# A four-layer graph network on one core: twenty summed rows a turn, GpSimd's signed blocks as maximum times sign, and layer norms scaled by VectorE

## The chip, the cores and the metric

The kernel runs on one core of one Trainium2 chip. The metric is the device time of one execution in microseconds (us). The kernel before takes 5407.69 us, the median of three runs (5406.17 to 5408.93).

## The reference, cut to what matters

64 graphs (batches) of 256 nodes with 128 features go through four layers, each `x = x + layer(relu(layernorm(x)))`. The first layer, a pairwise attention, is by far the largest piece of work:

```python
h = jnp.maximum(_layernorm(x, axis=-1), 0.0)
s1, s2 = einsum('bkf,ef->bke', h, W1), einsum('bkf,ef->bke', h, W2)   # e has 256 channels; W1 and W2 are halves of adj
pre = s1[:, :, None, :] + s2[:, None, :, :] + b_lin                    # 256 x 256 x 256 values a graph
e = einsum('bije,e->bij', where(pre >= 0, pre, 0.2 * pre), a) + adj
x = x + sigmoid(einsum('bij,bjf->bif', softmax(e, axis=2), h))
```

Layers 2 to 4 are a message-passing layer, an attention layer and a gated recurrent layer of five steps. They are small beside the first.

## The kernel before, in words

Two graphs (a pair) are worked through per *turn*; 32 turns carry the first layer, and layers 2 to 4 of earlier pairs run in their gaps. A turn has 128 *lots* (`LOTS`), 64 for each graph. In layer 1 the leaky slope is split off, so that what is left of each row i and channel half c is `max(W, U_i)`: W is a 128 x 256 tile (channels on partitions, all nodes j along the free axis) and U_i is one column. One such 128 x 256 maximum is a *block*. A lot is eight blocks, four groups of two halves (`BLOCKS`), which go into one of twelve places of `ring` (each four tiles of 128 x 512). TensorE then multiplies the place with `a_window` (L1163): four matmuls of 32 columns each, side by side, each of them two passes in the profile, so eight matmul rows for a lot.

The blocks of a lot are shared out by hand among three engines: VectorE (DVE; L746 for one block, L751 for two or four in one instruction), GpSimd (POOL; L620) and ScalarE (ACT; L956). `Plan.share_blocks` does it greedily with a price for each block and each stage (L89 and `stage_costs`, in tenths of a us), so that the three engines' running sums stay level. Each engine's program is in order: per lot its blocks, then the stages of the other layers that are booked at that lot (the tables `POST`, `PRE`, `LN1` to `LN3`, `L1` to `L3`). An engine that refills a place waits for `freed` of that place, which TensorE raises after the matmuls of the lot twelve before. TensorE waits for `by_dve`, `by_act` and `by_pool` of the place.

*Summed rows.* For some rows (`SUMMED_ROWS`, six of 32, 2 x 6 = 12 a turn over its two graphs) both channel halves are added ahead of the matmul, so that such a row needs one lot instead of two; from turn 2 on a turn has 116 lots instead of 128. The sign of the second half relative to the first is a column `sigma` of plus and minus ones. GpSimd makes the *signed* block, sigma times the maximum (L610), as a clamp of `W_signed` between `U_floor` and `U_ceiling`; these are made from `U_signed` in L599 and L600, and `U_signed` and `W_signed` by ScalarE in L976 and L979. VectorE then does maximum and addition in one instruction (L742), always by VectorE, four blocks a summed lot. `signed` has two buffers of four blocks.

*Layer norms.* For each graph (`pre`) and for LN1 to LN3 of a pair VectorE takes the statistics (L767, L772, L802, L808), minus the mean (L776, L812) and the variance plus epsilon (L777, L813). GpSimd makes the power -1/2 (L582) and the product of it and minus the mean (L584). ScalarE scales, shifts and clips each 128 x 128 block at zero in one activation (L964 for `pre`, two blocks; L1006 for the others, four blocks). TensorE transposes the result and ScalarE copies the transpose out of PSUM (L968, L1014, L1041, L1061).

## Time and profile before

| what | value |
|---|---|
| median of three runs | 5407.69 us (5406.17 to 5408.93) |
| the profiled execution | 5412.65 us, its span 5410.9 us |
| matmul, busy | 5288.8 us (98%), 37702 instructions |
| VectorE, busy | 5225.0 us (97%), 10763 |
| ScalarE, busy | 5143.4 us (95%), 13517 |
| GpSimd, busy | 5080.7 us (94%), 9752 |
| granted TensorE clock | 0.996 of full speed |

All four engines are busy over nine tenths of the span in nearly every slice. The profiled execution lies 5 us over the median of the runs. A busy time is the union of an engine's instructions; neighbours on one engine overlap a little, so the mean length of an instruction is more than what one more of it costs. The steady part of the execution repeats with every turn: L982, which runs once for each graph, starts at 1617.99 us and, 40 executions and so 20 turns later, at 4931.72 us, which is 165.69 us a turn.

### The profile page before, as it was taken

What the parts mean: (1) busy time and instruction counts of PE and PEld (TensorE: products, weight loads), DVE (VectorE), ACT (ScalarE), POOL (GpSimd) and SP (SyncE); (2) the same over time, 40 slices, a digit from 0 to 9 for tenths busy, and PEclk for the clock granted to TensorE, in tenths of its full rate; (3) what the DMA queues carried; (4) which work ended last, traced back from release to release, by engine and by line L of the source; (5) the groups of instructions that cost most, each with busy time, mean ns of one, the idle gap of its engine ahead of it and who ended that gap; (6) DMA issues with size and microseconds to landing.
All of it is one profiled execution on the core that took longest, in us unless ns stands there. A gap on an engine that the chain in (4) does not pass through costs nothing.

```text
span 5410.9 us, 115261 instructions
## 1 busy us (share of the span) xinstructions
PE 5288.8 (98%) x37702; PEld 2060.9 (38%) x37702; DVE 5225.0 (97%) x10763; ACT 5143.4 (95%) x13517; POOL 5080.7 (94%) x9752
## 2 busy tenths in 40 slices
PE   8999999999999999999999999999999999999997
PEld 2333333333333333333334333333333333333334
DVE  9999999999999999999999999999999999999993
ACT  8999999999999999999999999999999999999993
POOL 8899999999999999999999999999999999999990
PEclk9999999999999999999999999999999999999998
DMA  0000000000000000000000000000000000000000
GB/s 15 3 4 7 7 6 3 6 7 7 6 7 3 6 7 7 6 3 6 7 7 6 7 3 6 7 7 6 3 6 7 7 6 7 3 6 7 7 5 6
DMA packets 44381, 34.00 MB, mean 6 GB/s; under 512 B 4752, under 2 KB 39696, under 8 KB 43792
## 3 DMA queue, kind: packets, MB, share of 16 engines
q1 hardware_dynamic: 43792, 26.63, 1.6%
q8 instruction: 311, 5.10, 0.4%
q14 instruction: 278, 2.28, 0.1%
HBM read 9.84 MB, written 8.39 MB: 3 GB/s over the span
## 4 chain that ended last, share of the span: by engine, by line
PE 52%; ACT 26%; DVE 20%; issue 2%; DMA 0%; POOL 0%; SPq 0%; DVEq 0%; POOLq 0%
PE S L1163 29%; ACT ring L956 20%; PE R L1108 9%; DVE ring L751 8%; PE S L1108 5%; DVE ring L742 4%; PE W L1108 3%; DVE ring L746 2%; PE R L1301 2%; PE V L1108 1%; ACT h L1006 1%; DVE rh L890 1%; DVE gated L898 1%; DVE diff L894 1%; DVE h3T L902 1%
## 5 line engine op out<-in xcount | busy, mean ns | idle before, releaser
L956 ACT ACTIVATE ring<-V,U_minus 128x256 f32<-128x256 f32 x10681 | 4338.4, 850 | 1.6 <-issue 1.6
L1163 PE MATMUL S<-ring,a_window 128*32 128x512 f32 x29888 | 3401.9, 596 | 51.0 <-DVE ring L746 21.4
L620 POOL TENSOR_SCALAR ring<-W,U 128x256 f32<-128x256 f32 x6362 | 3175.7, 518 | 12.1 <-ACT V L982 11.8
L751 DVE TENSOR_TENSOR ring<-U,W 128x512 f32<-128x512 f32 (+1 forms) x2884 | 2536.1, 903 | 7.3 <-ACT V L982 7.3
L1163 PEld LDWEIGHTS S<-ring,a_window 128*32 128x32 f32 x29888 | 886.5, 109 | 2294.5 <-issue 2052.1
L610 POOL TENSOR_SCALAR signed<-W_signed,U_ceiling,U_floor 128x256 f32<-128x256 f32 x2880 | 1699.6, 594 | 6.3
L742 DVE SCALAR_TENSOR_TENSOR ring<-W,U,signed 128x256 f32<-128x256 f32 x2880 | 1193.8, 471 | 0.0
L746 DVE TENSOR_TENSOR ring<-U,W 128x256 f32<-128x256 f32 x1747 | 711.4, 409 | 0.0
L1108 PE MATMUL R<-mT,W 128*128 128x512 f32 (+1 forms) x640 | 334.9, 605 | 16.3 <-ACT mT L1068 16.3
L1108 PE MATMUL R<-AT,h 128*128 128x256 f32 x1264 | 311.9, 390 | 2.1 <-ACT h L1080 2.1
L582 POOL TENSOR_TENSOR rstd<-var,minus_half 128x4 f32<-128x4 f32 (+1 forms) x160 | 144.0, 900 | 141.2 <-DVE var L813 125.6
L1108 PEld LDWEIGHTS R<-AT,h 128*128 128x128 f32 x1264 | 230.6, 193 | 78.4 <-issue 50.3
L890 DVE SCALAR_TENSOR_TENSOR rh<-tr,h3T 128x512 f32<-128x512 f32 (+1 forms) x164 | 165.1, 1007 | 58.3 <-ACT tr L1071 58.3
L1074 ACT ACTIVATE tz<-R,bias 128x512 f32<-128x512 f32 (+1 forms) x160 | 161.1, 1007 | 52.4 <-PE R L1301 52.3
L1006 ACT ACTIVATE h<-X,shift,rstd 128x128 f32<-128x128 f32 x384 | 193.8, 870 | 6.8 <-POOL shift L584 6.8
L1080 ACT ACTIVATE h<-R 128x512 f32<-128x512 f32 (+1 forms) x128 | 131.8, 1029 | 69.5 <-PE R L1309 69.5
L1108 PEld LDWEIGHTS R<-mT,W 128*128 128x128 f32 x640 | 110.5, 192 | 172.0 <-ACT mT L1068 93.7
L1068 ACT ACTIVATE mT<-R 128x512 f32<-128x512 f32 (+1 forms) x160 | 165.0, 1031 | 11.0 <-PE R L1108 11.0
L1301 PE MATMUL R<-mT,W 128*128 128x512 f32 (+1 forms) x320 | 168.5, 608 | 0.0
L1071 ACT ACTIVATE tr<-R,bias 128x512 f32<-128x512 f32 (+1 forms) x160 | 157.6, 985 | 9.6 <-PE R L1108 9.6
L1077 ACT ACTIVATE cand<-R,bias 128x512 f32<-128x512 f32 (+1 forms) x160 | 164.7, 1029 | 0.7 <-PE R L1108 0.7
L1108 PE MATMUL R<-h3T,turned 128*128 128x512 f32 (+1 forms) x320 | 162.6, 590 | 0.0
(185 smaller groups left out, 4512.9 us busy)
## 6 DMA issues: line engine op xcount, KB each, us to landing
X<-in_x SPq DMA_DIRECT2D x64, 128.0 KB, 2.1
X_held<-X SPq DMA_DIRECT2D x32, 256.0 KB, 2.3
out<-OUT SPq DMA_DIRECT2D x64, 128.0 KB, 1.9
edge<-in_L_gnn_w_w SPq DMA_DIRECT2D x3, 128.0 KB, 2.2
A<-in_adj SPq DMA_DIRECT2D x1, 256.0 KB, 2.7
Wn<-in_L_gnn_Wn SPq DMA_DIRECT2D x1, 128.0 KB, 2.9
Wm<-in_L_gnn_Wm SPq DMA_DIRECT2D x1, 128.0 KB, 3.0
weight<-in_L_gnn_u_w SPq DMA_DIRECT2D x2, 64.0 KB, 2.2
```

What stands on the lines that cost most here:

```text
L610: made = gp.tensor_scalar(signed[:, number % 2, at], W_signed[:, y], U_ceiling[:, y, i:i + 1], U_floor[:, y, i:i + 1], ALU.min, ALU.max)
L620: last = gp.tensor_scalar(ring[:, place, g, half * N:(half + 1) * N], W[:, y, c], LARGEST, U[:, y, c, i:i + 1], ALU.min, ALU.max)
L742: piece = dve.scalar_tensor_tensor(ring[:, place, g, half * N:(half + 1) * N], w, U[:, y, c, i:i + 1], signed[:, number % 2, at], ALU.max, ...
L746: piece = dve.tensor_tensor(ring[:, place, g, half * N:(half + 1) * N], U[:, y, c, i:i + 1].to_broadcast([P, N]), w, ALU.max)
L751: piece = dve.tensor_tensor(ring[:, place, g:g + groups].rearrange("p g (h j) -> p g h j", h=NB), u.unsqueeze(3).to_broadcast([P, groups, ...
L890: dve.scalar_tensor_tensor(rh[:, cols_], tr[:, cols_], 1.0, h3T[:, cols_], ALU.add, ALU.mult).then_inc(rh_ready, 1)
L956: last = act.activation(ring[:, place, g, half * N:(half + 1) * N], W_scalar[y][:, c * N:(c + 1) * N], ACT.Relu, bias=U_minus[:, y, c, i:i ...
L1006: last = act.activation(dst[:, r], src[:, r], ACT.Relu, bias=shift[:, n, r:r + 1], scale=rstd[:, n, r:r + 1])
L1068: act.activation(mT[:, cols_], messages[:, cols_], ACT.Copy).then_inc(mT_ready, 1)
L1108: return pe.matmul(dst, lhsT, rhs, start=start, stop=stop)
L1163: last = pe.matmul(S[y][g * ROWS:(g + 1) * ROWS, :], a_window[:, c, ROWS - 1 - row:2 * ROWS - 1 - row], ring[:, place, g], start=False, st ...
L1301: pe.matmul(gates[:, cols_], W345[:, 0], mT[:, cols_], start=False, stop=True, skip_group_check=True).then_inc(z_psum, 1)
```

## The change

Three things change. First, ten rows of 32 are summed instead of six (`SUMMED_COUNT = 10`, twenty a turn): from turn 2 on a turn has 108 lots. The two sides of a lot begin at rows 22 and 21, so that their summed lots do not meet. Secondly, GpSimd makes a signed block from `W` and `U` directly, as maximum with `U_i`, then times `sigma`; the clamps, `U_signed`, `W_signed` and what they need go, and `signed` has three buffers. Thirdly, a layer norm's subtraction and scaling move from ScalarE to VectorE, one instruction per 128 x 128 block with two per-partition scalars. For LN1 and LN2 the clip at zero goes into ScalarE's copy out of PSUM; for `pre` and LN3 it is one more VectorE instruction over the whole tile. GpSimd makes the power only. The planner's stage prices follow, and its block prices stay.

```diff
-SUMMED_EVERY, SUMMED_AT = 5, 2
-SUMMED_ROWS = [row for row in range(ROWS) if row % SUMMED_EVERY == SUMMED_AT]
-FIRST_ROW = (0, 30)
+SIGNED = 3
+SUMMED_COUNT = 10
+SUMMED_ROWS = [(2 * n + 1) * ROWS // (2 * SUMMED_COUNT) for n in range(SUMMED_COUNT)]
+FIRST_ROW = (22, 21)
...
-            put(vector, PRE[h], half, stats=7.0)
-            put(scalar, PRE[h], half, norm=7.7, copy=2.7, evacuate=32)
-            put(pool, PRE[h], half, factors=12)
-            if self.has_sums:
-                book(pool, half, 11)
+            put(vector, PRE[h], half, stats=6.1, norm=6.6)
+            put(scalar, PRE[h], half, copy=2.7, evacuate=26)
+            put(pool, PRE[h], half, factors=8)
         if self.turn:
             for ln in (LN1, LN2, LN3):
-                put(vector, ln, 0, stats=12.5)
-                put(scalar, ln, 0, norm=15.4, copy=4.8)
-                put(pool, ln, 0, factors=12)
+                put(vector, ln, 0, stats=11.3, norm=11.8 if ln is LN3 else 7.9)
+                put(scalar, ln, 0, copy=4.8)
+                put(pool, ln, 0, factors=10)
...
                 gp.tensor_tensor(rstd_, var_, minus_half[:, 0:width], ALU.pow).then_inc(sem_rstd, 1)
-                gp.wait_ge(sem_rstd, value)
-                gp.tensor_tensor(shift_, minus_mean_, rstd_, ALU.mult).then_inc(sem_shift, 1)
...
-                    if turn.plan.has_sums:
-                        gp.tensor_scalar(U_floor[:, y], U_signed[:, y], sigma_limit[:], None, ALU.min)
-                        gp.tensor_scalar(U_ceiling[:, y], U_signed[:, y], sigma_limit[:], None, ALU.max).then_inc(clamps_ready, 1)
...
-                    if at == 0 and number >= 2:
-                        taken = divmod(number - 2, len(turn.plan.sum_lots))
+                    if at == 0 and number >= SIGNED:
+                        taken = divmod(number - SIGNED, len(turn.plan.sum_lots))
...
-                    made = gp.tensor_scalar(signed[:, number % 2, at], W_signed[:, y], U_ceiling[:, y, i:i + 1], U_floor[:, y, i:i + 1], ALU.min, ALU.max)
+                    made = gp.tensor_scalar(signed[:, number % SIGNED, at], W[:, y, 1], U[:, y, 1, i:i + 1], sigma[:], ALU.max, ALU.mult)
...
-                    dve.tensor_scalar(minus_mean0[:], mv0[:, :, 0], -1.0, None, ALU.mult)
                     dve.tensor_scalar(var0[:], mv0[:, :, 1], LN_EPS, None, ALU.add).then_inc(pre_eps, 1)
+                if p == PRE[1 - y]["norm"]:
+                    dve.wait_ge(pre_rstd, value)
+                    for r in range(NB):
+                        last = dve.tensor_scalar(H0[:, y, r], X0[:, y, r], mv0[:, r, 0:1], rstd0[:, r:r + 1], ALU.subtract, ALU.mult)
+                    last.then_inc(pre_scaled, 1)
+                    one_piece()
+                    dve.wait_ge(pre_scaled, value)
+                    dve.tensor_scalar(H0[:, y], H0[:, y], 0.0, None, ALU.max).then_inc(h0_ready, 1)
...
-                    dve.tensor_scalar(minus_mean[:, n], mv[:, n, :, 0], -1.0, None, ALU.mult)
+                if t == ln["norm"]:
+                    dve.wait_ge(ln_rstd[n], pair)
+                    for r in range(4):
+                        last = dve.tensor_scalar(dst[:, r], src[:, r], mv[:, n, r, 0:1], rstd[:, n, r:r + 1], ALU.subtract, ALU.mult)
+                    if n < 2:
+                        last.then_inc(h_ready[n], 1)
+                    else:
+                        last.then_inc(ln3_scaled, 1)
+                        one_piece()
+                        dve.wait_ge(ln3_scaled, pair)
+                        dve.tensor_scalar(dst[:], dst[:], 0.0, None, ALU.max).then_inc(h_ready[n], 1)
...
-                        last = act.activation(H0[:, y, r], X0[:, y, r], ACT.Relu, bias=shift0[:, r:r + 1], scale=rstd0[:, r:r + 1])
...
-                    act.activation(U_signed[:, y].rearrange("p (b k) -> p b k", k=len(SUMMED_ROWS)),
...
-                    act.activation(W_signed[:, y], W_bank[y][:, N:2 * N], ACT.Identity, scale=sigma[:])
...
-                        last = act.activation(dst[:, r], src[:, r], ACT.Relu, bias=shift[:, n, r:r + 1], scale=rstd[:, n, r:r + 1])
...
-                    act.activation(h1T[:], S[1][:], ACT.Copy).then_inc(hT_ready[0], 1)
+                    act.activation(h1T[:], S[1][:], ACT.Relu).then_inc(hT_ready[0], 1)
...
-                    act.activation(h2T[:], W_bank[0][:], ACT.Copy).then_inc(hT_ready[1], 1)
+                    act.activation(h2T[:], W_bank[0][:], ACT.Relu).then_inc(hT_ready[1], 1)
```

## Rows read from the trace of the kernel before

**Rows 1.** The page's busy times by engine, and its chain that ended last.
```profile
PE 5288.8 (98%) x37702; PEld 2060.9 (38%) x37702; DVE 5225.0 (97%) x10763; ACT 5143.4 (95%) x13517; POOL 5080.7 (94%) x9752
PE 52%; ACT 26%; DVE 20%; issue 2%; DMA 0%; POOL 0%; SPq 0%; DVEq 0%; POOLq 0%
```
**Rows 2.** Busy us per engine in a stretch of ten turns: PE, PEld, DVE, ACT, POOL.
```profile
1644.00:3301.00 1657.00, 1635.40 (x11701) 635.68 (x11700) 1630.99 (x3361) 1604.82 (x4223) 1605.19 (x3062) 1.00 0.02 6
```
**Rows 3.** Groups of the whole span: busy us, mean ns | idle before, releaser.
```profile
L956 ACT ACTIVATE ring<-V,U_minus 128x256 f32<-128x256 f32 x10681 | 4338.4, 850 | 1.6 <-issue 1.6
L1163 PE MATMUL S<-ring,a_window 128*32 128x512 f32 x29888 | 3401.9, 596 | 51.0 <-DVE ring L746 21.4 <-issue 21.2 <-ACT ring L956 3.1
L620 POOL TENSOR_SCALAR ring<-W,U 128x256 f32<-128x256 f32 x6362 | 3175.7, 518 | 12.1 <-ACT V L982 11.8 <-issue 0.3
L610 POOL TENSOR_SCALAR signed<-W_signed,U_ceiling,U_floor 128x256 f32<-128x256 f32 x2880 | 1699.6, 594 | 6.3
L751 DVE TENSOR_TENSOR ring<-U,W 128x1024 f32<-128x1024 f32 x1225 | 1455.0, 1211 | 0.0
L742 DVE SCALAR_TENSOR_TENSOR ring<-W,U,signed 128x256 f32<-128x256 f32 x2880 | 1193.8, 471 | 0.0
L751 DVE TENSOR_TENSOR ring<-U,W 128x512 f32<-128x512 f32 x1659 | 1110.3, 675 | 7.3 <-ACT V L982 7.3
L746 DVE TENSOR_TENSOR ring<-U,W 128x256 f32<-128x256 f32 x1747 | 711.4, 409 | 0.0
```
**Rows 4.** Some of the waits of the same ten turns: us in total, times, longest.
```profile
PEld S L1163 <- DVE ring L746: 40.8, 41, 1.4
POOL edge_sum L635 <- DVE edge L840: 23.6, 10, 2.5
POOL rstd L582 <- DVE var L813: 21.4, 30, 1.7
ACT h L1080 <- PE R L1309: 16.7, 20, 1.4
DVE X L850 <- PE S L1108: 13.0, 10, 1.3
```
**Rows 5.** Timeline, from the start, of back-to-back runs on three engines (start us, us).
```profile
2399.94 7.08 PE L1163 MATMUL S<-ring,a_window 128*32 128x512 f32 x64
...
2400.23 1.65 DVE L742 SCALAR_TENSOR_TENSOR ring<-W,U,signed 128x256 f32<-128x256 f32 x4
...
2410.20 2.78 PE L1163 MATMUL S<-ring,a_window 128*32 128x512 f32 x24
```
**Rows 6.** From the longest pieces of the critical chain: start us, us.
```profile
1630.34 6.93 ACT ring L956 x19
```
**Rows 7.** Two groups of the ten turns that the change removes.
```profile
L599 POOL TENSOR_SCALAR U_floor<-U_signed,sigma_limit 128x48 f32<-128x48 f32 x20 | 8.4, 419 | 0.0
...
L584 POOL TENSOR_TENSOR shift<-minus_mean,rstd 128x4 f32<-128x4 f32 x30 | 6.0, 199 | 2.3
```
**Rows 8.** Timeline: ScalarE's evacuation at the start, and one layer norm at the end.
```profile
15.04 0.41 ACT L976 ACTIVATE U_signed<-V,sigma_b,sigma 128x48 f32<-128x48 f32 x1
...
15.67 0.63 ACT L980 ACTIVATE W<-W 128x512 f32<-128x512 f32 x1
...
5318.31 1.65 ACT L1006 ACTIVATE h<-X,shift,rstd 128x128 f32<-128x128 f32 x4 [2.44 <-POOL shift L584]
```
**Rows 9.** VectorE's instructions with one SBUF input, whole span, by form.
```profile
L813 DVE TENSOR_SCALAR var<-mv 128x4 f32<-128x4 f32 x96 | 16.3, 170 | 0.0
...
L670 DVE TENSOR_SCALAR neg_score<-A,a_abs 128x256 f32<-128x256 f32 x2 | 0.6, 350 | 0.0
```
**Rows 10.** Timeline of VectorE and GpSimd side by side: L610 under L818.
```profile
2503.58 0.43 DVE L818 TENSOR_SCALAR exp<-exp 128x512 f32<-128x512 f32 x1
2503.66 0.77 POOL L610 TENSOR_SCALAR signed<-W_signed,U_ceiling,U_floor 128x256 f32<-128x256 f32 x1
```
**Rows 11.** L610 by itself: duration ns min/median/max.
```profile
L610 POOL TENSOR_SCALAR signed<-W_signed,U_ceiling,U_floor x2880: 539/553/1602, 301.8 to 5264.1; 128x256 f32<-128x256 f32 x192
```

More of the change, by code:

```diff
@@ L219, in spare_blocks @@
         for h in range(2):
-            for at in (POST[h]["transpose"], PRE[h]["stats"], PRE[h]["stats"]):
+            for at in (POST[h]["transpose"], PRE[h]["stats"], PRE[h]["stats"], PRE[h]["norm"]):
                 spare[h * LOTS_B + at] += 1
@@ L223, in spare_blocks @@
             spare[ln["stats"]] += 2
+        spare[LN3["norm"]] += 1
         for at in (L1["elu"], L1["recv_elu"], L2["residual"]):
@@ L258, in node @@
         return half * P + g * ROWS + self.entry(t, n)[0]
-    def signed_node(self, t, n):
-        g, half = group_half(n)
-        return (half * GROUPS + g) * len(SUMMED_ROWS) + SUMMED_ROWS.index(self.entry(t, n)[0])
 PLANS = [Plan(turn) for turn in range(3)]
@@ L369, in gnn_stack @@
         U_minus = sb("U_minus", [P, 2, EC, N])
[L370 to L374 removed]
+        signed = sb("signed", [P, SIGNED, SIDE_BLOCKS, N])
         W = sb("W", [P, 2, EC, N])
@@ L449, in gnn_stack @@
         freed = [sem(f"freed{n}") for n in range(RING)]
-        x_loaded, pre_stats, pre_mv, pre_eps, pre_rstd = (sem(n) for n in "x_loaded pre_stats pre_mv pre_eps pre_rstd".split())
-        pre_shift, h0_ready, h0T_psum, h0T_ready = (sem(n) for n in "pre_shift h0_ready h0T_psum h0T_ready".split())
-        clamps_ready, signed_ready = sem("clamps_ready"), sem("signed_ready")
+        x_loaded, pre_stats, pre_mv, pre_eps, pre_rstd, pre_scaled = (sem(n) for n in "x_loaded pre_stats pre_mv pre_eps pre_rstd pre_scaled".split())
+        h0_ready, h0T_psum, h0T_ready = (sem(n) for n in "h0_ready h0T_psum h0T_ready".split())
+        signed_ready = sem("signed_ready")
         uw_psum, u_ready, w_ready, u_evacuated = (sem(n) for n in "uw_psum u_ready w_ready u_evacuated".split())
@@ L463, in gnn_stack @@
         ln_rstd = [sem(f"ln{n}_rstd") for n in (1, 2, 3)]
-        ln_shift = [sem(f"ln{n}_shift") for n in (1, 2, 3)]
+        ln3_scaled = sem("ln3_scaled")
         h_ready = [sem(f"h{n}_ready") for n in (1, 2, 3)]
@@ L742, in one_piece @@
                     piece = dve.scalar_tensor_tensor(ring[:, place, g, half * N:(half + 1) * N], w, U[:, y, c, i:i + 1],
-                                                     signed[:, number % 2, at], ALU.max, ALU.add)
+                                                     signed[:, number % SIGNED, at], ALU.max, ALU.add)
                 elif end - first == 1:
@@ L826, in layer1 @@
                     dve.wait_ge(x1_ready, turn.at(2, 0))
-                stats(t, LN1, 0, X1, pair)
+                layer_norm(t, LN1, 0, X1, h1, pair)
                 if t == L1["elu"]:
@@ L881, in layer3 @@
                         dve.wait_ge(x3_ready, turn.at(1, 0))
-                    stats(t, LN3, 2, X3, turn.at(1, 0))
+                    layer_norm(t, LN3, 2, X3, h3, turn.at(1, 0))
                 pair, s, p = layer3_at(turn, t)
@@ L913, in _ @@
             pre(PRE[1]["stats"], 0, 1)
+            pre(PRE[1]["norm"], 0, 1)
             setup_layer0()
@@ L960, in pre @@
             def pre(p, y, value):
-                if p == PRE[1 - y]["norm"]:
-                    act.wait_ge(pre_shift, value)
-                    for r in range(NB):
-                        last = act.activation(H0[:, y, r], X0[:, y, r], ACT.Relu, bias=shift0[:, r:r + 1], scale=rstd0[:, r:r + 1])
-                    last.then_inc(h0_ready, 1)
                 if p == PRE[1 - y]["copy"]:
@@ L999, in post @@
                     last.then_inc(tanh0_ready, 1)
-            def norm(t, ln, n, src, dst, pair):
-                if t == ln["norm"]:
-                    act.wait_ge(ln_shift[n], pair)
-                    for r in range(4):
-                        last = act.activation(dst[:, r], src[:, r], ACT.Relu, bias=shift[:, n, r:r + 1], scale=rstd[:, n, r:r + 1])
-                    last.then_inc(h_ready[n], 1)
             def layer1(t, turn):
                 pair = turn.at(1, 0)
-                norm(t, LN1, 0, X1, h1, pair)
                 if t == LN1["copy"]:
                     act.wait_ge(hT_psum[0], pair)
-                    act.activation(h1T[:], S[1][:], ACT.Copy).then_inc(hT_ready[0], 1)
+                    act.activation(h1T[:], S[1][:], ACT.Relu).then_inc(hT_ready[0], 1)
                 if t == L1["exp"]:
@@ L1057, in layer3 @@
                 if turn.has_l12:
-                    norm(t, LN3, 2, X3, h3, turn.at(1, 0))
                     if t == LN3["copy"]:
```

37 lines of the change are left out of this document (9 added, 28 removed).

## The prediction

> **What bounds the kernel now.** I read the page first, then a stretch of whole turns, then who waited for whom. The page shows four engines busy for 94 to 98% of the span, and a chain that runs half over the matmuls [rows 1]. That alone would name TensorE as the bound, and the change would then be a gain, since it takes matmuls away. The rows on the ring say otherwise. If TensorE set the pace, the three engines that fill the ring would stand before a place that isn't free yet. In the whole span the five forms of ring instruction have idle time before them of 1.6 (ScalarE), 12.1 (GpSimd), 7.3, 0 and 0 us (VectorE), and the two large ones of these are one wait each for L982, at the very start [rows 3]. No fill ever waits for `freed`. The other way round there are waits: in ten turns TensorE's weight loads of the ring wait 41 times, 40.8 us in all, for VectorE's block [rows 4]. So the three filling engines set the pace and TensorE follows. Its own work shows it too: 64 ring matmuls back to back take 7.08 us and 24 take 2.78 [rows 5], so one costs 4.30 / 40 = 0.1075 us and a lot of eight 0.86 us; a turn of 116 lots is 99.8 us of ring matmul, where the busy time of L1163 is 3401.9 us over some 32 turns, 106 us each [rows 3]. About 6 us a turn of what looks busy is waiting under latency.
>
> How full are the three? In ten turns, 1657 us, VectorE is busy 1631.0, ScalarE 1604.8 and GpSimd 1605.2 us [rows 2]: per turn of 165.7 us that leaves 2.6, 5.2 and 5.2 us idle (rounded). Of GpSimd's 5.2 us, 2.4 + 2.1 are waits for VectorE (L840, L813) [rows 4]. VectorE is the fullest; 1.3 of its 2.6 us are a wait for a matmul of layer 2 (L850) [rows 4]. ScalarE waits for matmuls too, the largest 1.7 us a turn (L1080) [rows 4]. These waits are all that a lighter TensorE can give back.
>
> **The counts.** Followed through with the new constants, `share_blocks` gives for a turn from turn 2 on: summed blocks on VectorE 96 to 160, plain VectorE blocks in instructions of four 38 to 25, of two 50 to 34, of one 52 to 46; GpSimd's plain blocks 194 to 131, its signed blocks 96 to 160; ScalarE's blocks 334 to 359. The old counts agree with the trace: 30 x 96 = 2880 L742 and 2880 L610 [rows 3]. Turns 0 and 1 have no sums and change by under 2 us together.
>
> **TensorE.** Eight lots fewer: 8 x 0.86 = 6.9 us a turn less, 206 us over 30 turns. I put this at nothing, because it is work beside the filling engines; it only moves TensorE's slack from some 6 to some 13 us a turn.
>
> **VectorE, blocks.** Four L742 take 1.65 us together and one 0.471 [rows 3, 5], so the next one starts after 0.393 us: neighbours overlap by 0.08 us. With the same overlap off the means of [rows 3], an instruction of four blocks costs 1.13, of two 0.60, of one 0.33 us. The change: -13 x 1.13 - 16 x 0.60 - 6 x 0.33 + 64 x 0.393 = -14.7 - 9.6 - 2.0 + 25.2 = -1.1 us a turn.
>
> **VectorE, layer norms.** Sixteen instructions of 128 x 128 with two column scalars (four in `pre`, twelve in LN1 to LN3), two clips of 128 x 256 and one of 128 x 512. None of that form is in the trace. One of 4 elements takes 0.170 us, one of 256 with one column scalar 0.350 [rows 9], and one of 512 without 0.43 [rows 10]. Halfway between the first two is 0.26 for 128 elements; a second column scalar may add something; less the overlap that is 0.18 to 0.27, and I take 0.22, near the middle. The clips: 0.23 and 0.36. Sum 16 x 0.22 + 2 x 0.23 + 0.36 = 4.3 us. Five small instructions for minus the mean go, at 0.09 each (0.170 less the overlap) [rows 9], 0.5 us. Net +3.8 us, bounds +3.1 and +4.6. The new waits for `rstd` I price at nothing: in 30 cases GpSimd waited for VectorE's variance [rows 4], so it arrives two lots ahead and makes its power (mean about 1 us) before VectorE has done the next lot or two; if that lead is lost, each costs up to 1 us with all of VectorE's later pieces behind it, and L1's projection too.
>
> VectorE in all: +2.7 us a turn, 163.1 to 165.8.
>
> **ScalarE.** 19 blocks of L956 take 6.93 us [rows 6], 0.365 each: +25 x 0.365 = +9.1. Four L1006 take 1.65 us [rows 8]; with the last one's 0.5 off, the other three starts are 0.38 apart: -16 x 0.38 = -6.1. L976 and L979 take the 0.63 us from 15.04 to 15.67 [rows 8], twice a turn: -1.3. Net +1.7, from 160.5 to 162.2 us; not the bound.
>
> **GpSimd.** With busy time by count from [rows 3], L620 costs 3175.7 / 6362 = 0.50 and L610 1699.6 / 2880 = 0.59: -63 x 0.50 + 64 x 0.59 = +6.3. Four clamps go at 0.42, and five products at 0.2 [rows 7]: -1.7 - 1.0. That is +3.6. This takes the new signed block, a maximum and a multiplication with two column scalars, at the price of the old, a minimum and a maximum with two. The nearest rows bound it: L620, with one column scalar, at 0.50 is a low end, and as much above L610, 0.68, a high one, which is 160 x 0.09 = 14 us a turn either way, the most sensitive term. Downwards it stops mattering at once, since VectorE is then the bound; upwards it counts in full. I take the old price: same shape, same number of operands.
>
> Then there is contention. L610 has a median of 0.553 us [rows 11], and takes 0.77 when it lies under VectorE's one-input L818 of 0.43 us [rows 10]: it lost 0.22, half of the VectorE instruction. The new norms and clips are of that form, some 4.9 us a turn with their ends, so GpSimd loses about 2.4 us, between 0 and 4.9. GpSimd in all +6.0, 160.5 to 166.5.
>
> The Trainium skill (Advanced Engine Details and Errata, VectorE Performance Modes, Mode Summary) says that VectorE's second SBUF port is shared with GpSimd and that two-port VectorE instructions and GpSimd's block each other; by this rule one-input fp32 instructions between SBUF tiles, the norms among them, stop GpSimd for their whole length, where the row shows half. It speaks against moving the norms; what it would make of the time is the second rival.
>
> **The sum.** VectorE has 165.8 us of work and keeps some 1.8 of its 2.6 us idle (the wait at L850 shortens when TensorE is less behind): 167.6. GpSimd has 166.5, and of its 5.2 us of waiting for VectorE some 3.3 go, since it now comes 3.3 us later relative to VectorE: 168.4. Two engines at about the same level: I take 168.1 us, +2.4 a turn on 165.7. Over 30 turns +72 us; the end of the execution has three norms on its chain that get about 0.7 us shorter each, the beginning gains and loses under 1 us: -2. On the profiled execution's 5412.65 us that is 5483; the same +70 on the median of the runs gives 5478 us, 1.3% slower. The planner's own prices, which are in the code, point the same way: its fullest engine goes from 156.3 to 158.7 us a turn.
>
> **Rivals.**
> *TensorE's relief pays it back (0.22).* The waits for matmuls go entirely (VectorE 1.3 us, ScalarE's 1.7 and the smaller ones), the norms cost their low end, and GpSimd's extra work falls wholly into the time it now waits. Then VectorE has 163.1 - 1.1 + 3.1 + 1.3 idle = 166.4, or 165.0 if even its last idle time goes. For it: the chain runs 52% over matmuls [rows 1]. Against it: no fill waits for a free place [rows 3]. Time: 5385 to 5430 us; about half of this is faster than before by over 0.2%, a good third within it.
> *GpSimd becomes the bound (0.15).* The norms stop it for their full 4.9 us, or the signed block with a multiplication costs 0.03 us more (4.8 us a turn): 169 to 173.5 us a turn, 5510 to 5645 us. It decides from the point where GpSimd's work passes VectorE's 167.6. For it: L610's longest is 1.6 us, three times its median [rows 11]. Against it: most are at the median.
> *Waits inside the norms (0.05).* VectorE reaches its `norm` lot before GpSimd has the power, mostly at LN1, where one lot lies between; five waits of 0.5 to 1 us a turn on top of the sum: 5550 to 5630 us. For it: GpSimd gets more work and loses its lead. Against it: today it is the one that waits.
> *The sum as worked out (0.58):* 5440 to 5530 us.
>
> **The range.** 5405 to 5580 us: it leaves out the lower half of the first rival and the upper half of the two slower ones. About 0.2% (11 us) is what a measurement of this kernel can tell from no change. Faster by more 0.12, within it 0.10, slower 0.78.
>
> **What would show it.** After the change: the turn between executions of L982 is about 168 us instead of 165.7; L1163 has 27968 matmuls, its idle time and the waits of the weight loads for VectorE's blocks grow from 4 us a turn to some 9; ring fills still wait for nothing; L610's mean stays near 0.59 us and that of GpSimd's ring block rises slightly; the new norms have means near 0.3 us; VectorE is busy 98% or more. Wrong would be: ring fills that wait for `freed` in the steady part, or a turn under 165.7 us, which would mean that TensorE was the bound after all; a mean of the signed block away from 0.59 us by more than 0.03; waits of VectorE for `rstd` or `signed_ready`.

## The result

The changed kernel takes 8448.73 us, the median of four runs (8445.84 to 8456.74), where the kernel before took 5408.31 beside it: a ratio of 1.562, with a 95% interval of 1.559 to 1.565. The prediction was 5478 us with a range of 5405 to 5580. The direction was right and the size was not: 3040 us more, where 70 were foretold.

### The profile after

First the page of the changed kernel: busy times by engine, the granted clock by fortieths, the chain that ended last, and its costliest groups (busy us, mean ns | idle before, releaser).

```profile
span 8449.8 us, 112717 instructions
PE 6196.8 (73%) x35782; PEld 2111.2 (25%) x35782; DVE 5376.7 (64%) x12085; ACT 5268.4 (62%) x13651; POOL 8280.3 (98%) x9502
...
PEclk9988888889988988889888888888888888888888
...
POOL 94%; DVE 2%; PE 1%; ACT 1%; issue 1%; DMA 0%; DVEq 0%; POOLq 0%; SPq 0%
...
L586 POOL TENSOR_SCALAR signed<-W,U,sigma 128x256 f32<-128x256 f32 x4800 | 5990.3, 1253 | 0.8
L1136 PE MATMUL S<-ring,a_window 128*32 128x512 f32 x27968 | 4017.7, 676 | 2143.7 <-POOL ring L596 2064.0
L716 DVE SCALAR_TENSOR_TENSOR ring<-W,U,signed 128x256 f32<-128x256 f32 x4800 | 2002.4, 477 | 2661.7 <-POOL signed L586 2660.8
L596 POOL TENSOR_SCALAR ring<-W,U 128x256 f32<-128x256 f32 x4472 | 2132.7, 484 | 12.7 <-ACT V L966 12.7
```

Before, four engines were over 90% busy and the chain ran over three of them [rows 1]. Now only GpSimd is, at 98%, and 94% of the chain lies on it. VectorE stands 2661 us before L716 and waits for the signed block; before, that instruction never stood [rows 3]. The groups give the cause at once: L610, the old signed block, took a mean of 594 ns [rows 3], and L586, the new one, takes 1253. The plain block on GpSimd hardly moved, from 518 to 484 ns.

The second view is the one of L586 by itself (duration ns min/median/max), the third the busy time in a stretch of ten turns, in the order PE, PEld, DVE, ACT, POOL.

```profile
L586 POOL TENSOR_SCALAR signed<-W,U,sigma x4800: 1207/1214/2246, 299.7 to 8311.2; 128x256 f32<-128x256 f32 x192
```

```profile
2016.00:4687.00 2671.00, 1935.77 (x11057) 653.56 (x11060) 1677.78 (x3788) 1646.77 (x4266) 2670.70 (x2979) 0.88 0.01 4
```

The minimum is 1207 and the median 1214 ns, against a median of 553 for L610 [rows 11]. So this isn't contention, which would spread the values; each one costs 0.66 us more. 160 x 0.66 is 106 us a turn, a little more than the turn grew, since GpSimd gave up the 5.2 us a turn that it used to wait. The turn, from one pair's L966 to the next, is 267.1 us instead of 165.7, 101.4 us more, and 30 x 101.4 = 3042 us, where 3040 were measured. In ten turns GpSimd is busy for 2670.7 of 2671 us; before, 1605.2 of 1657 [rows 2].

The granted clock of TensorE fell from a mean of 0.996 of full speed to 0.883. In the same execution TensorE had 2143.7 us of idle time before the ring matmuls, 2064.0 of them for GpSimd. The lower clock isn't what makes the kernel slow, since GpSimd, which has 94% of the chain, doesn't wait for TensorE; that it fell because TensorE stood idle is a reading that wasn't tested.

### The profile page after: what moved, and what is told of

The parts are those of the page before. It is cut to its first block, busy times and chain, and to the rows that moved or that the text cites. A ratio compares the mean times of both kernels' runs of the same rounds, so it can differ in the third digit from the quotient of the medians.

```text
span 8449.8 us, 112717 instructions
## 1 busy us (share of the span) xinstructions
PE 6196.8 (73%) x35782; PEld 2111.2 (25%) x35782; DVE 5376.7 (64%) x12085; ACT 5268.4 (62%) x13651; POOL 8280.3 (98%) x9502
## 4 chain that ended last, share of the span: by engine, by line
POOL 94%; DVE 2%; PE 1%; ACT 1%; issue 1%; DMA 0%; DVEq 0%; POOLq 0%; SPq 0%
POOL signed L586 70%; POOL ring L596 22%; POOL rstd L565 2%; DVE ring L725 1%; ACT ring L949 1%; POOL X_shifted L608 0%; POOL edge_sum L611 0%; PE R L1081 0%; DVE ring L720 0%; PE S L1081 0%; PE S L1136 0%; DVE h L798 0%; PE W L1081 0%; DVE gated L890 0%; DVE diff L886 0%
## 5 line engine op out<-in xcount | busy, mean ns | idle before, releaser
L586 POOL TENSOR_SCALAR signed<-W,U,sigma 128x256 f32<-128x256 f32 x4800 | 5990.3, 1253 | 0.8
L1136 PE MATMUL S<-ring,a_window 128*32 128x512 f32 x27968 | 4017.7, 676 | 2143.7 <-POOL ring L596 2064.0
L716 DVE SCALAR_TENSOR_TENSOR ring<-W,U,signed 128x256 f32<-128x256 f32 x4800 | 2002.4, 477 | 2661.7 <-POOL signed L586 2660.8
L596 POOL TENSOR_SCALAR ring<-W,U 128x256 f32<-128x256 f32 x4472 | 2132.7, 484 | 12.7 <-ACT V L966 12.7
L1136 PEld LDWEIGHTS S<-ring,a_window 128*32 128x32 f32 x27968 | 740.9, 114 | 4953.9 <-issue 4756.0
L725 DVE TENSOR_TENSOR ring<-U,W 128x512 f32<-128x512 f32 (+1 forms) x2018 | 1771.8, 895 | 6.7 <-ACT V L966 6.6
L720 DVE TENSOR_TENSOR ring<-U,W 128x256 f32<-128x256 f32 x1569 | 639.2, 412 | 0.0
L1081 PE MATMUL R<-mT,W 128*128 128x512 f32 (+1 forms) x640 | 380.9, 681 | 2.7 <-ACT mT L1041 2.7
L798 DVE TENSOR_SCALAR h<-X,mv,rstd 128x128 f32<-128x128 f32 x384 | 137.1, 434 | 181.2 <-POOL rstd L565 181.2
L1274 PE MATMUL R<-mT,W 128*128 128x512 f32 (+1 forms) x320 | 177.4, 637 | 0.0
L1081 PE MATMUL R<-rh,turned 128*128 128x512 f32 (+1 forms) x320 | 167.5, 606 | 0.0
```

What stands on the lines that cost most here:

```text
L586: made = gp.tensor_scalar(signed[:, number % SIGNED, at], W[:, y, 1], U[:, y, 1, i:i + 1], sigma[:], ALU.max, ALU.mult)
L596: last = gp.tensor_scalar(ring[:, place, g, half * N:(half + 1) * N], W[:, y, c], LARGEST, U[:, y, c, i:i + 1], ALU.min, ALU.max)
L716: piece = dve.scalar_tensor_tensor(ring[:, place, g, half * N:(half + 1) * N], w, U[:, y, c, i:i + 1], signed[:, number % SIGNED, at], ALU ...
L720: piece = dve.tensor_tensor(ring[:, place, g, half * N:(half + 1) * N], U[:, y, c, i:i + 1].to_broadcast([P, N]), w, ALU.max)
L725: piece = dve.tensor_tensor(ring[:, place, g:g + groups].rearrange("p g (h j) -> p g h j", h=NB), u.unsqueeze(3).to_broadcast([P, groups, ...
L798: last = dve.tensor_scalar(dst[:, r], src[:, r], mv[:, n, r, 0:1], rstd[:, n, r:r + 1], ALU.subtract, ALU.mult)
```

## The experiments

The first question was which of three differences between L610 and L586 makes it slow: the pair of operations, the operands (`W` and `U` with a column of another tile, instead of three tiles made for it), or VectorE's new norms beside it. The second was whether the rest of the prediction's sum holds once that term is right. The third was whether its reading of the bound was right.

### Price lists: `forms` and `forms2`

Each form runs eight times over 128 x 256, in one execution for each list, for example:

```diff
+            for n in range(REPS):
+                last = gp.tensor_scalar(block[1][:, n], w[:, 1], u[:, n:n + 1], sigma[:], ALU.min, ALU.max)
+            for n in range(REPS):
+                last = gp.tensor_scalar(block[2][:, n], w[:, 1], u[:, n:n + 1], sigma[:], ALU.max, ALU.mult)
```

> Only a price list: GpSimd runs thirteen forms of a tensor_scalar over 128 x 256, eight of each, with the rest of the chip idle, then VectorE runs norms and clips alone, and at last GpSimd's old form and new form run beside VectorE's norms. Nothing of the layers is computed. Theory A, the operations are what costs: maximum then multiplication with two columns takes about 1.2 us alone, as in the changed kernel, and minimum then maximum with the same two columns about 0.55; then the forms with a multiplication, addition or subtraction tell which of them are dear. Theory B, the operands are (the column U beside a column of another tile): both take 1.2 us. Theory C, contention with VectorE's norms: both take about 0.55 us alone and the last eight over 1 us. For VectorE: a norm of 128 x 128 was put at 0.30 us in the prediction, the changed kernel shows 0.43; theory D, GpSimd beside it lengthens it, so 0.30 alone and over 0.4 beside GpSimd; theory E, two columns cost more than thought, 0.43 alone.

Rows of single lines of `forms` (duration ns min/median/max). L46 is the ring's form, minimum with a constant and then maximum with a column; L48 the old signed form; L50 the new one; L52 maximum and maximum; L54 one maximum alone; L68 multiplication and multiplication:

```profile
L46 POOL TENSOR_SCALAR block<-w,u x8: 473/474/474, 4.2 to 7.3; 128x256 f32<-128x256 f32 x8
...
L48 POOL TENSOR_SCALAR block<-w,u,sigma x8: 549/550/550, 7.8 to 11.5; 128x256 f32<-128x256 f32 x8
...
L50 POOL TENSOR_SCALAR block<-w,u,sigma x8: 1214/1214/1215, 12.1 to 20.4; 128x256 f32<-128x256 f32 x8
...
L52 POOL TENSOR_SCALAR block<-w,u,sigma x8: 1212/1212/1216, 21.6 to 30.0; 128x256 f32<-128x256 f32 x8
...
L54 POOL TENSOR_SCALAR block<-w,u x8: 912/917/921, 31.2 to 37.4; 128x256 f32<-128x256 f32 x8
...
L68 POOL TENSOR_SCALAR block<-w,sigma,u x8: 553/554/557, 92.9 to 96.6; 128x256 f32<-128x256 f32 x8
```

L48 and L50 read and write the same tiles, with nothing beside them: 550 against 1214 ns. So it is the pair of operations, and theories B and C are out. It isn't the multiplication: maximum with maximum costs the same 1212, and a single maximum, half the work, still 917.

> A second price list of GpSimd's tensor_scalar over 128 x 256, eight of each with the rest of the chip idle; nothing of the layers is computed. The first list had minimum then maximum at 0.47 to 0.55 us and multiplication then multiplication at 0.55, and all other pairs at 1.13 to 1.21, whatever the operands. Theory F, some pairs of operations are quick and all others slow: among maximum-minimum, minimum-minimum, multiplication-addition, subtraction-multiplication, addition-multiplication, addition-maximum, minimum-multiplication and multiplication-minimum most take 1.2 us and a few 0.55. Theory G, a maximum in the first place is what is slow: then minimum-minimum, multiplication-addition and the like all take 0.55 and maximum-minimum 1.2; against it already stands subtraction-maximum at 1.21.

```profile
L48 POOL TENSOR_SCALAR block<-w,u,sigma x8: 1222/1226/1231, 13.7 to 22.1; 128x256 f32<-128x256 f32 x8
...
L50 POOL TENSOR_SCALAR block<-w,u,sigma x8: 577/580/584, 23.3 to 27.1; 128x256 f32<-128x256 f32 x8
...
L54 POOL TENSOR_SCALAR block<-w,u,sigma x8: 601/608/614, 37.2 to 41.0; 128x256 f32<-128x256 f32 x8
```

Here L48 is minimum and minimum, L50 multiplication then addition, L54 addition then multiplication. Both lists together, medians in ns:

| pair (first, second) | two columns | one column and a constant |
|---|---|---|
| min, max | 550 | 474, 487 |
| mult, mult | 554 | 482 |
| mult, add | 580 | |
| add, mult | 608 | |
| max, mult; max, max; max, add; max, subtract; max, min | 1212 to 1219 | 1138, 1140 |
| mult, max; mult, min; min, mult; min, min | 1214 to 1241 | 1138, 1216 |
| subtract, max; subtract, mult; add, max | 1214 to 1284 | |
| max alone; mult alone | | 917; 922 |

Four pairs are quick and every other pair tried is slow, whatever it reads, with the single operations in between: theory F, and not G. The order counts too, since minimum then maximum is quick and maximum then minimum is not. The second column scalar costs some 60 to 80 ns in both classes (10 for minimum then multiplication). And more operations can be less time: one maximum alone takes 917 ns, and with a minimum against a huge constant in front of it, as the kernel's ring block has it, 474.

The rest of `forms` prices VectorE's norm: eight norms alone take 2.14 us with a mean of 342 ns, so they start 0.257 us apart. In the timeline:

```profile
106.20 2.14 DVE L84 TENSOR_SCALAR narrow<-w,u 128x128 f32<-128x128 f32 x8 [102.20 <-POOL block L70]
```

Of the two theories on the norm, D was the nearer, but 0.342 alone is already over its 0.30. Beside GpSimd's two signed forms (24 norms, L90) the median was still 0.353. The plain ring block was not run beside the norms in either list, and `before_norms` shows that it matters.

### The pair in its place: `after_max_max` and `before_mult`

```diff
-... W[:, y, 1], U[:, y, 1, i:i + 1], sigma[:], ALU.max, ALU.mult)
+... W[:, y, 1], U[:, y, 1, i:i + 1], sigma[:], ALU.max, ALU.max)
```

> The changed kernel with one word changed: the signed block is a maximum with U and then a maximum with sigma instead of a multiplication, so the first layer's scores are not the reference's. Theory A: the signed block is back at the price that the prediction took, 0.55 to 0.59 us, and the whole is what the prediction's sum gave, near 5478 us (5440 to 5530); if the sum's other terms are wrong too, it shows here without the one large error. Theory B (operands) and theory C (contention with the norms): no change, 8450 us.

8424.17 us, ratio 1.556 (1.552 to 1.559), mean of L586 1243 ns. What it foretold for theory A rested on the multiplication being at fault, and failed; the list above says why. It took the multiplication out of the question.

`before_mult` is the kernel before with the new signed block alone; the clamps and what they are made from go with it:

```diff
-... W_signed[:, y], U_ceiling[:, y, i:i + 1], U_floor[:, y, i:i + 1], ALU.min, ALU.max)
+... W[:, y, 1], U[:, y, 1, i:i + 1], sigma[:], ALU.max, ALU.mult)
```

> The kernel before, with its twelve summed rows and its norms on ScalarE, and GpSimd's signed blocks made as maximum times sign; the clamps and their sources go. 96 signed blocks a turn. Theory A: each costs 1.21 instead of 0.55 us, +63 us a turn less 1.7 for the clamps, GpSimd is the bound with about 160.5 + 61.5 = 222 us and few waits, so 5408 + 30 x 57 = 7120 us (7050 to 7250). Theory C: without the norms on VectorE nothing happens, 5400 us.

7104.23 us, ratio 1.311 (1.307 to 1.315), against 7120 expected. With no norm on VectorE and 96 signed blocks instead of 160 the same 1.24 us a block (the mean of its 2880) gives the time. The one instruction is enough by itself.

### What the prediction had priced: `after_min_max`

```diff
-... W[:, y, 1], U[:, y, 1, i:i + 1], sigma[:], ALU.max, ALU.mult)
+... W[:, y, 1], U[:, y, 1, i:i + 1], sigma[:], ALU.min, ALU.max)
```

> The changed kernel with its signed block as minimum with U, then maximum with sigma: the same operands, the pair of operations that the kernel before uses, and so another value in the first layer's scores. This is the kernel that the prediction priced. If the pair is all that was wrong: L586 at 0.55 to 0.59 us and the prediction's sum, 5478 us (5440 to 5530). If the norms, which cost VectorE 0.43 to 0.58 us each beside GpSimd instead of the 0.30 of the prediction, are short by 16 x 0.1 us a turn and more, it is 5500 to 5540. If the operands or the norms slow GpSimd, 8400 us.

5542.32 us, ratio 1.024 (1.021 to 1.026). So the pair accounts for 2906 of the 3040 us, and what is left, +2.4%, is still nearly twice the +1.3% of the sum. Ten turns (1700.7 us, 170.1 a turn; PE, PEld, DVE, ACT, POOL), and the groups in the same stretch:

```profile
1700.00:3400.70 1700.70, 1595.45 (x11062) 603.23 (x11060) 1696.64 (x3793) 1625.55 (x4275) 1653.18 (x2982) 0.99 0.02 6
```

```profile
L716 DVE SCALAR_TENSOR_TENSOR ring<-W,U,signed 128x256 f32<-128x256 f32 x1602 | 663.1, 469 | 0.0
...
L596 POOL TENSOR_SCALAR ring<-W,U 128x256 f32<-128x256 f32 x1312 | 679.1, 526 | 0.0
...
L798 DVE TENSOR_SCALAR h<-X,mv,rstd 128x128 f32<-128x128 f32 x120 | 57.1, 536 | 0.0
...
L754 DVE TENSOR_SCALAR H<-X,mv,rstd 128x128 f32<-128x128 f32 x40 | 17.6, 481 | 0.0
L758 DVE TENSOR_SCALAR H<-H 128x256 f32<-128x256 f32 x20 | 8.4, 419 | 0.0
```

Per turn VectorE is busy 169.7 us (predicted 165.8), ScalarE 162.6 (162.2) and GpSimd 165.3 (166.5). Two of three are within 1.2 us; VectorE is 3.9 over, and with 0.4 us idle a turn it is the bound. The sum had left it 1.8 us of idle time, so 1.4 us of waits that it counted did not come; the two errors together give 170.1 us a turn where the sum has 167.6 for VectorE. The norms are where it is: by busy time the sixteen of a turn take (57.1 + 17.6) / 10 = 7.5 us, where the sum has 16 x 0.22 = 3.5.

### The parts alone: `before_norms` and `clamped_10rows`

`before_norms` is the kernel before with the norms on VectorE, as in the change, and nothing else of it.

> The kernel before with the layer norms on VectorE alone, planner prices for the stages as in the change. By the prediction's terms: VectorE's norms +3.8 us and less blocks by the planner, ScalarE -6.1 and more blocks, GpSimd -1.0 and +2.4 by contention; shared out, about zero to +1 us a turn: 5400 to 5445 us. If the norms cost VectorE 0.43 us each as in the changed kernel, +2 us more on VectorE alone, 5440 to 5480. If VectorE stands before the power of GpSimd, it shows as idle time before the norms.

5456.6 us, ratio 1.009 (1.007 to 1.011): in the upper of the two ranges. VectorE didn't stand before the power; in the steady part its norms have no idle time before them. What lengthens a norm is to be seen beside GpSimd. First where one meets GpSimd's two-input instruction, L631, the X_shifted of layer 2 (timeline of `before_norms`: start us, us):

```profile
2508.22 1.29 POOL L631 TENSOR_TENSOR X_shifted<-X,bm_half 128x512 f32<-128x512 f32 x1
2508.22 2.42 DVE L823 TENSOR_SCALAR h<-X,mv,rstd 128x128 f32<-128x128 f32 x4
```

Both start at 2508.22. The four norms take 2.42 us where in `forms` four took 3 x 0.257 + 0.34 = 1.11: 1.31 us more, and GpSimd's instruction is 1.29 us long. The first of these four is a row of 1.37 us in every turn, the other three are 0.33 to 0.54. So VectorE's first norm lasted until GpSimd was through. The Trainium skill says that GpSimd's instructions and VectorE's two-port instructions block each other, and names a source and a destination in SBUF, as the norm has them, as a condition of the two-port mode (Advanced Engine Details and Errata, VectorE Performance Modes, Mode Summary). The trace agrees here, and VectorE is the one that pays: it lost 1.31 us to the 1.29 us of GpSimd's instruction.

That is one norm of sixteen. The rest of the loss lies beside GpSimd's plain block (`ring`, L619), which `forms` had not run beside a norm:

```profile
2456.65 3.15 POOL L619 TENSOR_SCALAR ring<-W,U 128x256 f32<-128x256 f32 x5
2458.95 1.92 DVE L823 TENSOR_SCALAR h<-X,mv,rstd 128x128 f32<-128x128 f32 x4
2459.79 0.55 POOL L609 TENSOR_SCALAR signed<-W_signed,U_ceiling,U_floor 128x256 f32<-128x256 f32 x1
2460.32 1.55 POOL L619 TENSOR_SCALAR ring<-W,U 128x256 f32<-128x256 f32 x3
```

No two-input instruction is near, and four norms still take 1.92 us instead of 1.11. Sorted by what GpSimd does during them, the norms of the ten turns from 1700 us have a median of 0.53 us where they met plain blocks alone (26 norms) and of 0.34, as long as alone, where they met signed blocks alone (32 norms). In `after_min_max` the 57 that met signed blocks alone have 0.39 and the 92 that met both kinds 0.54. So the kind of GpSimd block beside a norm goes with what it costs; no run has the plain block and the norms alone, and why they differ stays open.

`clamped_10rows` has the rows alone: the kernel before with

```diff
-RING = 12
+RING = 11
-SUMMED_EVERY, SUMMED_AT = 5, 2
-SUMMED_ROWS = [row for row in range(ROWS) if row % SUMMED_EVERY == SUMMED_AT]
-FIRST_ROW = (0, 30)
+SIGNED = 3
+SUMMED_EVERY, SUMMED_AT = 3, 1
+SUMMED_ROWS = [row for row in range(ROWS) if row % SUMMED_EVERY == SUMMED_AT][:10]
+FIRST_ROW = (22, 21)
```

and the third buffer of `signed`. The ring has eleven places here, to make room for the clamps' tiles of ten rows and the third buffer. That is a second difference beside the rows, but no fill of the ring waits for a free place in this run.

> The kernel before with ten rows of 32 summed (every third), three signed buffers and a ring of eleven places, norms on ScalarE as before, signed blocks by the clamp: the rows alone. clamped_norms_10rows is +3.8% and before_norms +0.9%; if they add, this is +2.9%, 5565 us. Counting: 64 signed blocks and 64 L742 more, 128 plain blocks less: 64 x 0.59 + 64 x 0.39 = 62.7 us of engine time against 15 us less for TensorE's sake nothing and 128 x 0.37 = 47, so 15.5 us over three engines, +5.2 us a turn, 5565 us as well.

5561.5 us, ratio 1.029 (1.028 to 1.031), against 5565 expected. Its ten turns take 1708.1 us:

```profile
1700.00:3408.10 1708.10, 1611.14 (x11073) 593.94 (x11076) 1653.64 (x3694) 1646.05 (x4326) 1650.86 (x3054) 1.00 0.02 6
```

Per turn the three filling engines are busy for 165.4 + 164.6 + 165.1 = 495.1 us, where before they were for 163.1 + 160.5 + 160.5 = 484.1 [rows 2]. That is 11.0 us more, 3.7 for each, and waits make up the rest of the 5.1 us that the turn got longer. TensorE has lost 2.4 us of busy time a turn, and the turn is longer all the same. In this kernel a summed row saves TensorE work and costs the filling engines more than they have to spare.

With both, `clamped_norms_10rows`:

> A correct version of two thirds of the change: ten rows of 32 summed (every third), norms on VectorE, three signed buffers, but the signed blocks by the old clamp; to fit, the ring has eleven places. The prediction's terms, with the clamps, U_signed and W_signed kept (+1.7 us on GpSimd, +1.3 on ScalarE): 5490 us (5460 to 5560). If eleven places are too few, fills wait for a free place.

5626.96 us, ratio 1.038 (1.037 to 1.040), 67 us over the upper end of what was expected. The 0.9% and 2.9% of the two parts add up to its 3.8%. Two of its waits are not among those of before, whole span (us, times, longest):

```profile
POOL signed L610 <- DVE ring L742: 119.9, 90, 1.9
DVE ring L742 <- POOL signed L610: 117.3, 59, 3.6
```

GpSimd waits for a free signed buffer and VectorE for a full one, in turns, 4 us a turn each. (Of the ring's fills one waits for a free place, 0.5 us in all, so the eleven places aren't the cause.) In `clamped_10rows` they are 50.2 and 149.9 us. The prediction had priced these waits at nothing. For the change itself that was nearly right: in `after_min_max` GpSimd's is 26.1 us in all, and VectorE has none. Why the kernels with clamps have more of them wasn't looked into.

### What TensorE is worth: `before_half_matmul`, `before_5rows`

```diff
-                    last = pe.matmul(S[y][g * ROWS:(g + 1) * ROWS, :], a_window[...],
-                                     ring[:, place, g], start=False, ...
+                    last = pe.matmul(S[y][g * ROWS:(g + 1) * ROWS, 0:N], a_window[...],
+                                     ring[:, place, g, 0:N], start=False, ...
```

> The kernel before with each ring matmul over 256 of its 512 columns, so half of each place goes into no score and the first layer's scores are wrong; every fill, wait and stage stays. TensorE has some 50 us a turn less. Theory H, the filling engines set the pace and TensorE's relief is worth the waits for it at most: VectorE's 1.3 us before L850 and some of ScalarE's, 5360 to 5410 us; TensorE's idle time grows by 50 us a turn. Theory I, TensorE sets the pace in the stretches where it runs back to back: the turn falls to what VectorE has to do, 163.1 us and a few tenths, 5330 us or less.

5318.74 us, ratio 0.984 (0.983 to 0.986): below theory H's range, 5360 to 5410, and within what theory I gave, 5330 or less. Busy times of the page, and ten turns (1628.2 us):

```profile
PE 4261.0 (80%) x37702; PEld 2038.1 (38%) x37702; DVE 5198.1 (98%) x10763; ACT 5136.6 (97%) x13517; POOL 5056.4 (95%) x9752
```

```profile
1600.00:3228.20 1628.20, 1318.21 (x11696) 631.19 (x11700) 1621.30 (x3361) 1601.15 (x4218) 1598.17 (x3064) 0.94 0.02 6
```

By the prediction's price of a matmul TensorE was relieved of half of its 99.8 us of ring matmul a turn; its busy time fell by 31.7 us, from 163.5 to 131.8, with the granted clock at 0.94 instead of 1.00. The turn has lost 2.9: 162.8 instead of 165.7. Then VectorE is busy for 1621.3 of 1628.2 us and has nothing left to give. So both theories have a part of it. As H has it, TensorE's relief is worth next to nothing: 50 us returned 6% of itself. As I has it, TensorE did hold the turn before, by 2.9 us, and the turn falls to what VectorE has to do. The prediction named 1.3 us of VectorE's waits for this; VectorE's idle time fell by 1.9 us, from 2.6 to 0.7, and its busy time by 1.0, from 163.1 to 162.1. The second part is as large as what one group lost: L890, which reads ScalarE's `tr`, went from 53.2 to 42.8 us in ten turns. This much relief of TensorE brings 87 us, 1.6%.

In the other direction, one summed row less (`SUMMED_EVERY, SUMMED_AT = 6, 2`):

> The kernel before with five rows of 32 summed instead of six, nothing else: 118 lots a turn. If the filling engines set the pace, fewer sums are cheaper: 16 signed blocks (0.59) and 16 L742 (0.39) go and 32 plain blocks come, at a joint rate of the three engines of 1 per 0.123 us: 15.7 us of engine time less, 11.6 more, a third of the difference is -1.3 us a turn, 5370 us. TensorE gets 1.7 us more a turn and has some 6. If TensorE sets the pace: +1.7 us a turn, 5460 us.

5462.73 us, ratio 1.008 (1.006 to 1.010). It went the way of the theory that TensorE sets the pace, and that theory's number, 5460, is met; the other, 5370, is missed. But the groups point to another cause. In ten turns VectorE is busy for as long as before, 1631.5 us, though it has 16 summed blocks a turn less to add:

```profile
1700.00:3373.90 1673.90, 1653.82 (x11861) 636.60 (x11860) 1631.48 (x3301) 1599.80 (x4200) 1596.17 (x3060) 1.00 0.02 6
```

and its idle time is 4.2 us a turn instead of 2.6. Its ring blocks fell by 1.3 us a turn, from 139.6 to 138.3, as the theory on the filling engines had it, and L890 by 1.2. But one group, L833 of layer 2, which reads two SBUF tiles, rose by 2.6, from 21.9 to 48.3 us in ten turns. One L833 of every turn is what grew (timelines of `before_5rows` and of `before`):

```profile
2031.45 5.24 POOL L620 TENSOR_SCALAR ring<-W,U 128x256 f32<-128x256 f32 x11
2032.93 2.95 DVE L833 CUSTOM_DVE_ANT_0 exp<-xh,We_src,be 128x128 f32<-128x128 f32 x1
```

```profile
2015.94 0.56 POOL L610 TENSOR_SCALAR signed<-W_signed,U_ceiling,U_floor 128x256 f32<-128x256 f32 x1
2016.40 0.70 DVE L833 CUSTOM_DVE_ANT_0 exp<-xh,We_src,be 128x128 f32<-128x128 f32 x1
2016.47 0.48 POOL L620 TENSOR_SCALAR ring<-W,U 128x256 f32<-128x256 f32 x1
2016.93 0.59 POOL L610 TENSOR_SCALAR signed<-W_signed,U_ceiling,U_floor 128x256 f32<-128x256 f32 x1
```

With other rows summed, seven plain blocks in a row now pass beside it, where before signed blocks stood between them. The kernel before has one such L833 too, of 2.64 us at 202.9 us, before the first signed block (301.8 us), and seven plain blocks pass beside that one as well. After it ScalarE's edge (L1026) waits 4.0 us a turn for L833 instead of 1.0, and VectorE waits 117.3 us in the whole span for ScalarE's tr (L1071), where before it waited 58.3. By these rows 5460 was met for a reason that was in neither theory. That the seven plain blocks are the cause is read off the traces; no run has them alone.

### Can the planner do it: `before_vector_repriced`, `after_signed_priced`

```diff
-            for costs, stages in ((vector, dict(update=7, state=18, out=6 ...
+            for costs, stages in ((vector, dict(update=9, state=21, out=6 ...
```

> The kernel before with two prices of the planner raised to what the trace shows: VectorE's update of the recurrent layer from 0.7 to 0.9 us and its state from 1.8 to 2.1 us. Per turn VectorE gets 5 blocks less, ScalarE 3 and GpSimd 2 more. If VectorE sets the pace: its 163.1 us fall by 1.5, ScalarE's and GpSimd's 160.5 rise by about 1.0, and the turn falls by 0.5 to 1.5 us, 5365 to 5395 us. If TensorE does: no change, 5410.

5422.27 us, ratio 1.003 (1.002 to 1.004): 0.3% slower, and neither theory's number. VectorE's busy time fell as meant, from 163.1 to 160.6 us a turn, and its waits took more than that back:

```profile
1700.00:3362.50 1662.50, 1640.65 (x11705) 630.72 (x11701) 1605.57 (x3321) 1616.53 (x4253) 1611.00 (x3081) 1.00 0.02 6
```

The idle time is now 5.7 us a turn. In the ten turns VectorE waits 17.0 us for ScalarE's exp (L1034) and 17.6 for its cand (L1077), where before it waited 3.0 and 0.6. The kernel before is balanced closely enough that less work on its fullest filling engine doesn't shorten it when the other two get it.

`after_signed_priced` is the changed kernel with `POOL_SIGNED` at 12.1 instead of 5.43, in tenths of a us.

> The changed kernel with the planner's price of a signed block at 1.21 us, which is what it costs. The planner can then take all plain blocks off GpSimd but no signed ones: 160 x 1.21 + its stages of 8 us = 202 us a turn, so GpSimd stays the bound, near 5408 + 30 x 37 = 6520 us. It tells how much of the loss is the pair of operations itself and how much the planner that did not know of it (8449 - 6520).

6477.62 us in its one run. Ten turns, 2015.8 us:

```profile
1900.00:3915.80 2015.80, 1703.34 (x11064) 590.00 (x11060) 1849.70 (x3941) 1835.53 (x4852) 2015.64 (x1671) 0.97 0.02 5
```

GpSimd is full with the signed blocks and its stages, without a plain block. Of the loss of 3040 us, 1971 come from a planner that went on at the old price, and 1069 remain with the right one.

## Why the prediction was wrong

By its own steps:

- *What bounds the kernel:* held in part. That TensorE's relief is worth little holds: it was put at the waits for matmuls, 1.3 us a turn of VectorE's, and is 2.9 us for seven times the relief that the change brings (50 us against 6.9). That VectorE's work sets the pace isn't shown: with 2.5 us a turn less of it, and 1.2 and 0.6 more on ScalarE and GpSimd, the turn got 0.6 us longer (`before_vector_repriced`). All four engines are within a few us of the turn, and the waits between them are as large as that.
- *TensorE, -206 us priced at nothing:* nearly held. L1163's successor has the 27968 matmuls foretold, and in `after_min_max`, where GpSimd is at its old price, TensorE is idle for 10.5 us a turn instead of 2.2, and the turn is longer. But of VectorE's idle time, of which the sum kept 1.8 us a turn, 0.4 is left there, so up to 1.4 us a turn may have come back by it.
- *VectorE, blocks, -1.1 us:* held. In `after_min_max` the error of VectorE's sum is in the norms.
- *GpSimd, the signed block at the old price:* **this step failed**. "Same shape, same number of operands" said nothing about the term that counts, the pair of operations, and none of the rows cited had a pair other than minimum and maximum. Measured: 1.214 us instead of 0.553, 106 us a turn, 2906 of the 3040 us. The upper bound, 0.68, had no row behind it; it was the lower one's distance, mirrored. In the trace of before, every GpSimd `tensor_scalar` of this size is one of L620 and L610, both minimum then maximum, so the trace could not have priced the new pair. The honest end of the range was open, and the list of things to watch for named it, "a mean of the signed block away from 0.59 us by more than 0.03".
- *With that term put right,* the prediction's own sum comes near the result. By count, as the 0.59 was taken, a block of the changed kernel costs 5990.3 / 4800 = 1.25 us, and GpSimd's 166.5 + 160 x (1.25 - 0.59) = 272 us a turn, measured 267.1. Of the difference 3 us are the plain blocks, 0.48 us each by count instead of 0.50.
- *VectorE, norms, +3.8 us:* the term was mis-sized. `after_min_max` has 3.9 us more on VectorE than the sum. A norm alone starts every 0.257 us instead of the 0.22 taken, 0.6 us of it. The rest shows where norms run beside GpSimd, the larger part of it beside plain blocks and the smaller beside X_shifted, and the prediction charged this contention to GpSimd alone. GpSimd's side was right (its plain block went from 0.503 to 0.518 us by count), but VectorE pays as well: 0.53 us for a norm of 0.34 beside plain blocks, and 1.37 beside X_shifted, both in `before_norms`.
- *ScalarE, +1.7 us:* held, 162.6 for 162.2.
- *Waits for `rstd` at nothing:* held in the steady part of `after_min_max` and `before_norms`. In the changed kernel itself they are there, 181.2 us at L798 and 94.9 at L754, because GpSimd is behind.
- *The rival "GpSimd becomes the bound"* named the mechanism, with a chance of 0.15, and gave 5510 to 5645 us. Its price, "0.03 us more", was twenty times too small.
- *The range:* the kernel that the sum priced, at 5542 us, would have lain inside 5405 to 5580, but with luck: VectorE's work was 3.9 us a turn too low and its idle time 1.4 too high, which partly cancel.

The Trainium skill has a model for GpSimd (GPSIMD Engine Reference, Elementwise — side-by-side cycle accounting) by which a loop body with up to two operations per element is bound by its read and write ports; which operations they are doesn't enter it. Here the measurement decides: with the same operands, a block of the same size written, and two operations per element in both, one takes 0.55 and the other 1.21 us.

## What to carry to other kernels

A price belongs to an instruction with its operations, not to its shape: where the trace has no row with the same pair of operations on the same engine, the upper end is open, and the first step is to time that instruction alone, eight of it in a row. On an engine that is 94% full and has 96 or 160 of them a turn, nothing else in the change matters beside it. And a hand-set price in a planner has to be measured again whenever the instruction it stands for is rewritten, because here two thirds of the loss came from blocks that the planner kept giving to an engine it took to be far less busy than it was. And a price measured with the other engines idle is a lower end: beside it must run what the kernel has beside it, as the plain blocks were missing beside the norms here.

## What the runs showed that was not expected

- GpSimd's `tensor_scalar` in fp32 over 128 x 256 has two classes: 0.47 to 0.61 us for min-max, mult-mult, mult-add and add-mult, and 1.14 to 1.28 us for the sixteen other two-operation forms timed. A single operation takes 0.92, twice the time of the same maximum with a minimum against a huge constant in front of it.
- GpSimd's instruction with two SBUF inputs (1.29 us) held VectorE's one-input norm for its whole length, 1.37 us for one that takes 0.34 alone. Its plain block (minimum with a constant, maximum with a column) went with a norm of 0.53 us, and its signed block (two columns) with one of 0.34 to 0.39. Beside seven plain blocks in a row VectorE's L833 took 2.95 us instead of 0.70.
- A kernel with all four engines 94 to 98% busy had 1.6% to gain from halving the largest piece of its fullest engine, TensorE.
